# Relative attention: the sheared bias stored, loaded and waited for tile by tile

## The chip, the cores and the metric

One core of one Trainium2 chip runs the whole program. The metric is the device time of one execution in microseconds (us). Five engines run their own instruction streams and meet only through counters (semaphores): TensorE (PE in the profile), VectorE (DVE), ScalarE (ACT), GpSimd (POOL) and SyncE (SP), which here only issues DMA transfers. "PE waits for a counter" means that its stream stands still, in order, until another engine or a landed transfer has raised it.

## What is computed

The program is an audio tower: a token convolution and then four layers, each an attention and a feed-forward part. The change touches one part, the attention of layer 0, with a learned bias that depends on the distance of two positions:

```python
qkv = group_norm(x @ W_qkv, gn_qkv_scale, gn_qkv_bias)      # 4 batches, 8 heads, L = 746 positions
rel_idx = jnp.arange(L)[:, None] - jnp.arange(L)[None, :] + (L - 1)
rpe = rel_emb[:, rel_idx]                                   # rpe_q, rpe_k, rpe_v are its parts
logits = (jnp.einsum('bhdi,bhdj->bhij', q, k) + jnp.einsum('bhdi,dij->bhij', q, rpe_k)
          + jnp.einsum('bhdi,dij->bhij', k, rpe_q))
attn = jax.nn.softmax(logits, axis=3)
out = (jnp.einsum('bhij,bhdj->bhdi', attn, v) + jnp.einsum('bhij,dij->bhdi', attn, rpe_v))
```

## The kernel before

`rel_attention` works through 32 pairs (batch, head). A pair is 6 tiles of 128 query rows (`T = 6`). The bias of row i at column j depends only on j - i, and only 4 tiles (`NS = SKEW_TILES = 4`) and the last 510, 382, 254 and 126 columns of them (`SKEW_W`) have one that differs from a constant. So TensorE makes it unsheared (`position`, L783, into the one bank `x_ps`), ScalarE copies it out (`copy_position`, L887, into `r_sb`), SyncE stores it to a scratch tensor in device memory (L721) and loads it back with a row step that is one short, which shifts each row by one (L735, into four buffers `bias[slot][t]`). VectorE adds it to the scores (L949), takes the row maximum (L953), ScalarE exponentiates (L909), VectorE scales by the reciprocal sum (L931, L933). The probabilities make the same trip in the other direction (L703 stores, L745 loads into `shear`), TensorE transposes both (`turn_probs` L807, `turn_shear` L820), ScalarE and VectorE copy the transposes out, and TensorE multiplies with the values (L834) and the value embedding (L845, the last work of a pair).

Three pairs are in flight. A call `body(new, now, old)` is one turn: `new` gets its bias (position products, stores, loads), `now` its scores and softmax, `old` its output. Two sets of buffers (`slot`) alternate, and every second turn also copies and stores the output of two pairs (L939 on VectorE, L710 on SyncE, four transfers). On each engine the order within a turn is written by hand and strictly kept. In a turn TensorE does in step t: transposes of tile t - 2, scores of tile t + 1, position product t, and from step 2 on parts of `old`. The scores of tile 0 of the next pair are issued in step 5, ahead of L820, L834 and L845. VectorE does in step t: add bias t (t < 4), maximum t, scale t - 1, copy of half a transpose (t >= 2).

Before the change SyncE stores all four tiles of a pair on one counter (`bias_out[slot]`), waits until all four have landed, then issues the four loads on one counter (`bias_in[slot]`), and VectorE waits for all four loads ahead of its first add:

```python
                if new is not None:
                    sp.wait_ge(bias_out[new.slot], new.turn * (16 * NS) + 16 * NS)
                    ...
                    for t in range(NS):
                        sp.dma_start(bias[new.slot][t][:], sheared("rel_bias", new.slot, t, SKEW_ROW - 1, SKEW_W[t])
                                     ).then_inc(bias_in[new.slot], 16)
```

`apart(eng, passed)` raises a counter that nobody waits for; it stands between two waits on one engine so that each has an instruction of its own.

## Time and profile before

| | |
|---|---|
| median of 3 runs | 3236.6 us (3222.63 to 3237.94) |
| profiled execution, its own time | 3237.81 us |
| its span in the profile | 3236.0 us |
| mean granted TensorE clock, whole span | 0.864 |
| relative attention, from the first position product (156.77 us) to the last output store issued (717.43 us) | 561 us of the span |

The span is the time between the first and the last instruction that the profiler saw; the execution's own time is 1.8 us longer. Times in rows are us from the start of the span. The granted clock is 1.00 at 2.4 GHz and 0.50 at 1.2 GHz. An idle time in brackets stands ahead of the instruction that ended it, with what released it. Idle time of an engine that others do not wait for costs nothing.

### The profile page before, as it was taken

How to read it: one execution, taken by the hardware profiler on the slowest of the kernel's cores; microseconds unless marked ns; L12 is line 12 of the kernel's file. 1: busy time of each engine (PE TensorE's matmuls, PEld its weight loads, DVE VectorE, ACT ScalarE, POOL GpSimd, SP SyncE). 2: the span in 40 equal slices, each digit the busy share in tenths (PEclk: the TensorE clock that was granted, in tenths of full speed). 3: DMA queues.
4: the chain of work that ended last, by engine and by line, in shares of the span. 5: the costliest groups of instructions: out<-in, count | busy, mean ns of one | idle time of the engine just before them, and what ended most of it. 6: DMA issues, size and time to landing. Idle time of an engine off the chain costs nothing. (4 is left out here: it accounts for less than half of the span.)

```text
span 3236.0 us, 47690 instructions
## 1 busy us (share of the span) xinstructions
PE 2579.5 (80%) x16218; PEld 1748.2 (54%) x16266; DVE 1705.1 (53%) x3666; ACT 1330.0 (41%) x2799; POOL 203.7 (6%) x240
## 2 busy tenths in 40 slices
PE   5389999975579947867886999998599999962973
PEld 3245555543467846644463666664366666642862
DVE  3477888753306503451353777776476767641113
ACT  2156777652104401433451554554155555531321
POOL 0000000000310040000000000000100000005022
PEclk8578999886789968877996999999699999975986
DMA  2345555542204510001004121320332323102651
GB/s 80 114 153 166 171 181 175 175 129 88 95 20 159 161 34 2 2 1 40 15 1 150 41 101 71 121 92 1 90 87 68 78 66 80 31 9 79 213 162 47
DMA packets 166565, 286.92 MB, mean 89 GB/s; under 512 B 44652, under 2 KB 125924, under 8 KB 162292
## 3 DMA queue, kind: packets, MB, share of 16 engines
q1 hardware_dynamic: 152900, 262.80, 25.7%
q0 software_dynamic: 6144, 12.60, 1.3%
q10 hardware_dynamic: 7360, 9.44, 1.0%
q8 instruction: 93, 1.52, 0.2%
q14 instruction: 68, 0.56, 0.1%
HBM read 167.71 MB, written 79.86 MB: 77 GB/s over the span
## 5 line engine op out<-in xcount | busy, mean ns | idle before, releaser
L2969 ACT ACTIVATE lstm_gate<-lstm_g_ps,lstm_bias 128x373 f32<-128x373 f32 x368 | 210.1, 574 | 251.2 <-PE lstm_g_ps L2930 236.4
L3568 DVE TENSOR_REDUCE caus_nmx<-caus_a_ps 128x4 f32<-128x512 f32 (+5 forms) x352 | 215.9, 642 | 106.2 <-PE caus_a_ps L3384 103.4
L2930 PE MATMUL lstm_g_ps<-lstm_state,lstm_w 128*128 128x373 f32 x640 | 254.7, 480 | 6.7 <-DVE lstm_state L3052 4.1
L3519 ACT ACTIVATE caus_probsT<-caus_s_ps 128x512 f32<-128x512 f32 (+4 forms) x352 | 189.7, 559 | 150.5 <-PE caus_s_ps L3403 147.0
L807 PE MATMUL rel_t_ps<-tower_ident,rel_probs 128*128 128x128 f32 x1152 | 189.1, 307 | 40.0 <-DVE rel_probs L933 36.5
L436 PE MATMUL moe_hb<-moe_z_part,moe_w1h 128*128 x576 | 156.4, 349 | 63.0 <-issue 53.3
L2924 PE MATMUL lstm_g_ps<-lstm_xm,lstm_w 128*128 128x373 f32 x512 | 202.3, 477 | 0.0
L953 DVE TENSOR_REDUCE rel_nmax<-rel_s_ps 128x1 f32<-128x746 f32 x192 | 179.0, 932 | 20.2 <-PE rel_s_ps L792 13.2
L3384 PE MATMUL caus_a_ps<-caus_ks,caus_qs 96*128 96x128 f32 (+6 forms) x768 | 180.6, 327 | 10.6 <-DVE caus_nmx L3568 10.4
L807 PEld LDWEIGHTS rel_t_ps<-tower_ident,rel_probs 128*128 128x128 f32 x1152 | 144.1, 156 | 80.4 <-DVE rel_probs L933 53.6
L3403 PE MATMUL caus_s_ps<-caus_qs,caus_ks 98*128 98x128 f32 (+6 forms) x768 | 186.4, 333 | 0.5 <-ACT caus_probsT L3519 0.4
L909 ACT ACTIVATE rel_probs<-rel_s_ps,rel_nmax 128x746 f32<-128x746 f32 x192 | 171.5, 893 | 22.2 <-DVE rel_rsum L931 11.9
L2930 PEld LDWEIGHTS lstm_g_ps<-lstm_state,lstm_w 128*128 128x128 f32 x640 | 122.1, 191 | 87.1 <-DVE lstm_state L3052 4.7
L696 ACT COPY rel_probsT<-rel_t_ps 128x384 f32<-128x384 f32 x256 | 117.4, 486 | 125.1 <-PE rel_t_ps L807 123.2
L436 PEld LDWEIGHTS moe_hb<-moe_z_part,moe_w1h 128*128 128x128 f32 x576 | 109.6, 199 | 67.9 <-issue 67.3
L3403 PEld LDWEIGHTS caus_s_ps<-caus_qs,caus_ks 98*128 98x128 f32 (+1 forms) x768 | 122.7, 190 | 34.5 <-issue 21.8
L3384 PEld LDWEIGHTS caus_a_ps<-caus_ks,caus_qs 96*128 96x128 f32 (+1 forms) x768 | 122.3, 191 | 30.3 <-DVE caus_nmx L3568 23.8
L1779 DVE SCALAR_TENSOR_TENSOR stage_y<-moe_ob,moe_b,tower_zT 128x373 f32<-128x373 f32 x8 | 4.8, 605 | 249.2 <-PE moe_ob L1579 249.2
L2203 ACT ACTIVATE moe_hid<-moe_hb,moe_w 128x256 f32<-128x256 f32 x152 | 62.4, 471 | 179.3 <-PE moe_hb L2139 91.4
L2924 PEld LDWEIGHTS lstm_g_ps<-lstm_xm,lstm_w 128*128 128x128 f32 x512 | 97.3, 190 | 63.1
L436 PE MATMUL moe_hb<-moe_z_part,moe_w1l 128*128 x288 | 99.9, 347 | 28.5 <-issue 28.5
L933 DVE TENSOR_SCALAR rel_probs<-rel_probs,rel_rsum 128x746 f32<-128x746 f32 x192 | 117.0, 609 | 6.8
(477 smaller groups left out, 5080.5 us busy)
## 6 DMA issues: line engine op xcount, KB each, us to landing
lstm_row<-gates SPq DMA_DIRECT2D x16, 1536.0 KB, 13.7
moe_w<-in_moe_w SPq DMA_DIRECT2D x38, 578.0 KB
moe_ew<-in_moe_w SPq DMA_DIRECT2D x33, 578.0 KB
caus_qs<-caus_xh SPq DMA_DIRECT2D x128, 93.2 KB, 2.1
caus_ks<-caus_xh SPq DMA_DIRECT2D x128, 93.2 KB, 2.1
lstm_row<-gates SPq DMA_DIRECT2D x8, 1152.0 KB, 7.3
moe_x<-moe_xs SPq DMA_DIRECT2D x71, 128.0 KB
moe_ys<-moe_yo SPq DMA_DIRECT2D x71, 128.0 KB, 1.7
```

What stands on the lines that cost most here:

```text
L436: mm = nc.tensor.matmul(out, w[i], x[j], start=(start and n == 0), stop=(stop and n == len(terms) - 1))
L696: copy(probsT[pair.slot][:, j0:j0 + T // 2, t * P:(t + 1) * P], t_ps[i][:, 0:T // 2 * P].rearrange("p (j i) -> p j i", i=P)).then_inc(t_co ...
L807: mm = nc.tensor.transpose(t_ps[i][:, j * P:(j + 1) * P], probs[pair.slot][:, t, k * P:(k + 1) * P], K["ident"][:])
L909: nc.scalar.activation(probs[now.slot][:, t, 0:L], s_ps[t % 2][:, 0:L], ACT.Exp, bias=nmax[now.slot][:, t:t + 1], accum_out=sums[now.slot] ...
L953: nc.vector.tensor_reduce(nmax[now.slot][:, t:t + 1], s_ps[t % 2][:, 0:L], AX.X, ALU.max, negate=True).then_inc(max_ready, 1)
L2924: mm = nc.tensor.matmul(bank, w[e % 2][:, g * P:(g + 1) * P], z, start=True, stop=(s == 0))
L2930: mm = nc.tensor.matmul(bank, w[e % 2][:, 4 * P + g * P:4 * P + (g + 1) * P], state[e % 2][k or 0][i][:], start=False, stop=True)
L2969: nc.scalar.activation(gate[x % 3][g][:], g_ps[n % RING][:, 0:HALF], ACT.Tanh if g == 2 else ACT.Sigmoid, bias=b[:, e, g:g + 1]).then_inc( ...
L3384: mm = nc.tensor.matmul(out[:, at, :], qs[s][0:K_S, hh, t * P:q1], ks[s][0:K_S, hh, k0:k1], start=not diag, stop=not diag or hh == HPG - 1)
L3403: mm = nc.tensor.matmul(out[:, at, :], ks[s][0:K_T, hh, j * P:k1], qs[s][0:K_T, hh, q0:q1], start=not diag, stop=not diag or hh == HPG - 1)
L3519: nc.scalar.activation(probsT[j][0:rows, heads[0]:heads[-1] + 1, q0 - j * P:q1 - j * P], heads_of(s_ps[at % 3][0:rows, :], heads, q1 - q0) ...
L3568: nc.vector.tensor_reduce(nmx[0:rows, slot, heads[0]:heads[-1] + 1, t:t + 1], heads_of(bank[0:rows, :], heads, k1 - k0), AX.X, ALU.max, ne ...
```

## The change

Each tile gets counters of its own. SyncE stores tile t, and then, once the store of tile t - 1 has landed, issues the load of tile t - 1; the last load comes behind the last store of probabilities. VectorE waits ahead of each of the four adds for that tile alone, ScalarE ahead of each of its four copies for the store that last read that part of `r_sb`. The wait for all four scores of `old` ahead of the loads is dropped; each load waits for `old`'s add of the same tile. The bytes moved and the work of all engines are the same. VectorE, ScalarE and SyncE get `apart` instructions and waits in each turn.

```diff
--- before.py
+++ after.py
@@ -650,7 +650,8 @@
         x_ps = a.ps("x_ps", [P, BANK])
         o_ps = a.ps("o_ps", [P, BANK])
         in_sem = a.sems("pair_in", 2)
-        bias_out, bias_in = a.sems("bias_out", 2), a.sems("bias_in", 2)
+        bias_out = [a.sems(f"bias_out{i}_", SKEW_TILES) for i in range(2)]
+        bias_in = [a.sems(f"bias_in{i}_", SKEW_TILES) for i in range(2)]
         probs_out, shear_in = a.sems("probs_out", 2), a.sems("shear_in", 2)
         t_copied = a.sems("t_copied", 2)
         names = ("r_full", "r_copied", "a_full", "a_copied", "s_full", "max_ready", "exp_done", "rs_ready",
@@ -703,6 +704,14 @@
                 sp.dma_start(scratch["rel_probs"][now.slot, t, :, 0:SKEW_W[t]],
                              probs[now.slot][:, t, L - SKEW_W[t]:L]).then_inc(probs_out[now.slot], 16)
 
+            def load_bias(new, old, t):
+                sp.wait_ge(bias_out[new.slot][t], new.turn * 16 + 16)
+                if old is not None:
+                    apart(sp, passed)
+                    sp.wait_ge(biased, old.n * ADDED + t + 1)
+                sp.dma_start(bias[new.slot][t][:], sheared("rel_bias", new.slot, t, SKEW_ROW - 1, SKEW_W[t])
+                             ).then_inc(bias_in[new.slot][t], 16)
+
             def store_output(turn):
                 sp.wait_ge(o_copied, turn + 1)
                 for q, c0 in enumerate(QUARTERS):
@@ -711,31 +720,27 @@
                                  o_sb[q * 2 * HD:(q + 1) * 2 * HD, 0:c1 - c0]).then_inc(o_stored, 16)
 
             def body(new, now, old):
-                if old is not None and new is not None:
-                    sp.wait_ge(bias_in[new.slot], new.turn * (16 * NS))
                 if old is not None and now is not None and not now.early:
                     sp.wait_ge(shear_in[now.slot], now.turn * (16 * NS))
+                    apart(sp, passed)
                 for t in range(NS):
                     if new is not None:
+                        if old is not None:
+                            sp.wait_ge(bias_in[new.slot][t], new.turn * 16)
+                            apart(sp, passed)
                         sp.wait_ge(r_copied, new.n * NS + t + 1)
                         sp.dma_start(scratch["rel_bias"][new.slot, t, :, 0:SKEW_W[t]], r_sb[new.slot][:, t, 0:SKEW_W[t]]
-                                     ).then_inc(bias_out[new.slot], 16)
+                                     ).then_inc(bias_out[new.slot][t], 16)
+                        if t > 0:
+                            load_bias(new, old, t - 1)
                     if now is not None and t > 0:
                         store_probs(now, t - 1)
                     if t == 2 and old is not None and old.slot == 0 and not old.first:
                         store_output(old.turn - 1)
-                if new is not None:
-                    sp.wait_ge(bias_out[new.slot], new.turn * (16 * NS) + 16 * NS)
-                    apart(sp, passed)
-                    if old is not None:
-                        sp.wait_ge(s_full, old.n * T + NS)
-                        apart(sp, passed)
-                        sp.wait_ge(biased, old.n * ADDED + ADDED)
-                    for t in range(NS):
-                        sp.dma_start(bias[new.slot][t][:], sheared("rel_bias", new.slot, t, SKEW_ROW - 1, SKEW_W[t])
-                                     ).then_inc(bias_in[new.slot], 16)
                 if now is not None:
                     store_probs(now, NS - 1)
+                if new is not None:
+                    load_bias(new, old, NS - 1)
                 if now is not None:
                     sp.wait_ge(probs_out[now.slot], now.turn * (16 * NS) + 16 * NS)
                     apart(sp, passed)
@@ -881,8 +886,9 @@
                 act.dma_start(rhs[pair.slot][:], scratch["rel_rhs"][bass.ds(pair.n, 1), :, :].squeeze(0)).then_inc(in_sem[pair.slot], 16)
 
             def copy_position(new, old, t):
-                if t == 0 and old is not None:
-                    act.wait_ge(bias_out[new.slot], new.turn * (16 * NS))
+                if old is not None:
+                    act.wait_ge(bias_out[new.slot][t], new.turn * 16)
+                    apart(act, passed)
                 act.wait_ge(r_full, new.n * NS + t + 1)
                 nc.scalar.copy(r_sb[new.slot][:, t, 0:SKEW_W[t]], x_ps[:, 0:SKEW_W[t]]).then_inc(r_copied, 1)
 
@@ -943,8 +949,8 @@
                     if now is not None:
                         dve.wait_ge(s_full, now.n * T + t + 1)
                         if t < ADDED:
-                            if t == 0:
-                                dve.wait_ge(bias_in[now.slot], now.turn * (16 * NS) + 16 * NS)
+                            apart(dve, passed)
+                            dve.wait_ge(bias_in[now.slot][t], now.turn * 16 + 16)
                             corner = s_ps[t % 2][:, L - SKEW_W[t]:L]
                             nc.vector.tensor_tensor(corner, corner, bias[now.slot][t][:], ALU.add).then_inc(biased, 1)
                             dve.wait_ge(biased, now.n * ADDED + t + 1)
```

SyncE, the straight-line turn behind the loop (pair 31 is `new`), before: `rel_r_sb` to `rel_bias` is a store of the bias, `rel_probs` to `rel_probs` a store of probabilities, `rel_bias_t` a load of tile t.

```order
L721 DMA rel_bias<-rel_r_sb 128x510 [waits rel_r_copied,rel_shear_in0,rel_bias_in1]
L721 DMA rel_bias<-rel_r_sb 128x382 [waits rel_r_copied]
L703 DMA rel_probs<-rel_probs 128x510 [waits rel_scaled]
L721 DMA rel_bias<-rel_r_sb 128x254 [waits rel_r_copied]
L703 DMA rel_probs<-rel_probs 128x382 [waits rel_scaled]
L721 DMA rel_bias<-rel_r_sb 128x126 [waits rel_r_copied]
L703 DMA rel_probs<-rel_probs 128x254 [waits rel_scaled]
L735 DMA rel_bias_0<-rel_bias 128x510 [waits rel_bias_out1,rel_s_full,rel_biased]
L735 DMA rel_bias_1<-rel_bias 128x382
L735 DMA rel_bias_2<-rel_bias 128x254
L735 DMA rel_bias_3<-rel_bias 128x126
L703 DMA rel_probs<-rel_probs 128x126 [waits rel_scaled]
```

The same turn, changed:

```order
L732 DMA rel_bias<-rel_r_sb 128x510 [waits rel_shear_in0,rel_bias_in1_0,rel_r_copied]
L732 DMA rel_bias<-rel_r_sb 128x382 [waits rel_bias_in1_1,rel_r_copied]
L712 DMA rel_bias_0<-rel_bias 128x510 [waits rel_bias_out1_0,rel_biased]
L704 DMA rel_probs<-rel_probs 128x510 [waits rel_scaled]
L732 DMA rel_bias<-rel_r_sb 128x254 [waits rel_bias_in1_2,rel_r_copied]
L712 DMA rel_bias_1<-rel_bias 128x382 [waits rel_bias_out1_1,rel_biased]
L704 DMA rel_probs<-rel_probs 128x382 [waits rel_scaled]
L732 DMA rel_bias<-rel_r_sb 128x126 [waits rel_bias_in1_3,rel_r_copied]
L712 DMA rel_bias_2<-rel_bias 128x254 [waits rel_bias_out1_2,rel_biased]
L704 DMA rel_probs<-rel_probs 128x254 [waits rel_scaled]
L704 DMA rel_probs<-rel_probs 128x126 [waits rel_scaled]
L712 DMA rel_bias_3<-rel_bias 128x126 [waits rel_bias_out1_3,rel_biased]
```

The load of tile 0 has moved from behind all stores of the bias to behind the second, ahead of the first store of probabilities, and waits for one landing; loads 1 and 2 stand each behind the next store, load 3 behind the last store of probabilities.

VectorE, the third turn (pair 1 is `now`), steps 0 to 2, before:

```order
L949 TENSOR_TENSOR rel_s_ps<-rel_s_ps,rel_bias_0 128x510 [waits rel_bias_in1,rel_s_full]
L953 TENSOR_REDUCE rel_nmax<-rel_s_ps 128x1 [waits rel_biased]
L931 RECIPROCAL rel_rsum<-rel_sums 128x1 [waits rel_exp_done]
L933 TENSOR_SCALAR rel_probs<-rel_probs,rel_rsum 128x746 [waits rel_rs_ready]
L949 TENSOR_TENSOR rel_s_ps<-rel_s_ps,rel_bias_1 128x382 [waits rel_s_full]
L953 TENSOR_REDUCE rel_nmax<-rel_s_ps 128x1 [waits rel_biased]
L931 RECIPROCAL rel_rsum<-rel_sums 128x1 [waits rel_exp_done]
L933 TENSOR_SCALAR rel_probs<-rel_probs,rel_rsum 128x746 [waits rel_rs_ready]
L949 TENSOR_TENSOR rel_s_ps<-rel_s_ps,rel_bias_2 128x254 [waits rel_s_full]
```

And changed:

```order
L955 TENSOR_TENSOR rel_s_ps<-rel_s_ps,rel_bias_0 128x510 [waits rel_s_full,rel_bias_in1_0]
L959 TENSOR_REDUCE rel_nmax<-rel_s_ps 128x1 [waits rel_biased]
L937 RECIPROCAL rel_rsum<-rel_sums 128x1 [waits rel_exp_done]
L939 TENSOR_SCALAR rel_probs<-rel_probs,rel_rsum 128x746 [waits rel_rs_ready]
L955 TENSOR_TENSOR rel_s_ps<-rel_s_ps,rel_bias_1 128x382 [waits rel_s_full,rel_bias_in1_1]
L959 TENSOR_REDUCE rel_nmax<-rel_s_ps 128x1 [waits rel_biased]
L937 RECIPROCAL rel_rsum<-rel_sums 128x1 [waits rel_exp_done]
L939 TENSOR_SCALAR rel_probs<-rel_probs,rel_rsum 128x746 [waits rel_rs_ready]
L955 TENSOR_TENSOR rel_s_ps<-rel_s_ps,rel_bias_2 128x254 [waits rel_s_full,rel_bias_in1_2]
```

Nothing has moved; the first add waits for one tile's counter, and the second and third (and the fourth, below) have a wait for a landing of their own beside that for the scores. The counter instructions of `apart` are not listed in this view.

## Rows read from the trace of the kernel before

**Rows 1.** Window: length, busy PE, PEld, DVE, ACT, POOL, clock, DMA share, GB/s.

```profile
160.00:720.00 560.00, 497.73 (x4093) 283.83 (x4093) 429.41 (x848) 375.41 (x894) 8.60 (x30) 0.88 0.52 164
```

**Rows 2.** Waits of the stage: us in total, times, longest.

```profile
DVE rel_s_ps L949 <- DMA rel_bias<-rel_bias: 76.0, 32, 12.7
PE rel_t_ps L807 <- DVE rel_probs L933: 36.5, 55, 2.2
```

**Rows 3.** Timeline, VectorE, end of one turn: start us, us, instruction, idle before.

```profile
421.11 0.55 DVE L696 COPY rel_probsT<-rel_t_ps 128x384 f32<-128x384 f32 x1
423.28 0.70 DVE L949 TENSOR_TENSOR rel_s_ps<-rel_s_ps,rel_bias 128x510 f32<-128x510 f32 x1 [1.62 <-DMA rel_bias<-rel_bias]
```

**Rows 4.** Timeline, SyncE's DMA issues, one turn.

```profile
411.66 2.33 SPq L721 DMA_DIRECT2D rel_bias<-rel_r_sb  x2
417.17 0.32 SPq L721 DMA_DIRECT2D rel_bias<-rel_r_sb  x1
419.04 1.75 SPq L735 DMA_DIRECT2D rel_bias<-rel_bias  x4
423.57 1.74 SPq L745 DMA_DIRECT2D rel_shear<-rel_probs  x4
```

**Rows 5.** Timeline, TensorE, the same turn and a row of the next.

```profile
408.14 0.87 PE L807 MATMUL rel_t_ps<-tower_ident,rel_probs 128*128 128x128 f32 x6
410.68 0.88 PE L807 MATMUL rel_t_ps<-tower_ident,rel_probs 128*128 128x128 f32 x6 [0.80 <-DVE rel_probs L933]
412.83 0.87 PE L807 MATMUL rel_t_ps<-tower_ident,rel_probs 128*128 128x128 f32 x6 [0.59 <-DVE rel_probs L933]
423.86 0.87 PE L807 MATMUL rel_t_ps<-tower_ident,rel_probs 128*128 128x128 f32 x6
429.93 0.66 PE L820 MATMUL rel_x_ps<-tower_ident,rel_shear 128*128 128x128 f32 x4
```

**Rows 6.** DMA issues by line: KB each, median us to landing.

```profile
rel_bias<-rel_r_sb SPq DMA_DIRECT2D x32, 255.0 KB, 2.0
rel_bias<-rel_bias SPq DMA_DIRECT2D x32, 255.0 KB, 2.6
```

**Rows 7.** Timeline, VectorE, then TensorE, a turn whose bias came early.

```profile
552.27 0.70 DVE L949 TENSOR_TENSOR rel_s_ps<-rel_s_ps,rel_bias 128x510 f32<-128x510 f32 x1 [0.48 <-DMA rel_bias<-rel_bias]
555.74 0.56 DVE L949 TENSOR_TENSOR rel_s_ps<-rel_s_ps,rel_bias 128x382 f32<-128x382 f32 x1 [1.00 <-PE rel_s_ps L792]
...
554.40 0.87 PE L807 MATMUL rel_t_ps<-tower_ident,rel_probs 128*128 128x128 f32 x6
558.04 0.87 PE L807 MATMUL rel_t_ps<-tower_ident,rel_probs 128*128 128x128 f32 x6 [0.39 <-DVE rel_probs L933]
569.33 0.88 PE L807 MATMUL rel_t_ps<-tower_ident,rel_probs 128*128 128x128 f32 x6
```

**Rows 8.** Timeline, TensorE: L845 of the first and the 31st pair.

```profile
200.30 1.36 PE L845 MATMUL rel_o_ps<-rel_shearT,rel_relv_pad 128*32 128x187 f32 x18
706.66 1.36 PE L845 MATMUL rel_o_ps<-rel_shearT,rel_relv_pad 128*32 128x187 f32 x18 [0.72 <-ACT rel_shearT L918]
```

**Rows 9.** Windows of 4 us, columns as in Rows 1.

```profile
341.00:345.00 4.00, 3.06 (x18) 1.51 (x17) 3.77 (x8) 3.03 (x8) 0.27 (x1) 1.00 0.58 179
345.00:349.00 4.00, 3.53 (x18) 1.80 (x19) 3.90 (x8) 2.65 (x7) 0.00 (x0) 0.52 0.48 180
554.40:558.40 4.00, 3.43 (x22) 2.05 (x22) 2.94 (x7) 3.41 (x8) 0.27 (x1) 1.00 0.56 188
```

**Rows 10.** Timeline, VectorE, the projection: an instruction behind a counter instruction.

```profile
125.35 0.21 DVE L461 BATCH_NORM_AGGREGATE relproj_qk_work<-relproj_qk_stats 128x2 f32<-128x12 f32 x1 [0.15 <-DVE relproj_qk_stats L459]
```

**Rows 11.** Timeline, start of the stage: SyncE, then VectorE.

```profile
158.00 2.89 SPq L721 DMA_DIRECT2D rel_bias<-rel_r_sb  x4
162.91 1.74 SPq L735 DMA_DIRECT2D rel_bias<-rel_bias  x4
...
167.17 0.70 DVE L949 TENSOR_TENSOR rel_s_ps<-rel_s_ps,rel_bias 128x510 f32<-128x510 f32 x1 [12.68 <-DMA rel_bias<-rel_bias]
```

## Prediction

> **What bounds the kernel now.** I read the page first, then the windows over the attention stage, the chain of waits inside it, and the timelines of VectorE, SyncE and TensorE side by side for single turns. The program is one of many stages in a row, with barriers between them, so the change is worth what it takes out of this one. In the stage no engine is full: of 560 us TensorE is busy 497.7, VectorE 429.4, ScalarE 375.4, and the granted clock averages 0.88, which is 0.24 x 560 = 134 us at 1.2 GHz [rows 1]. The wait list names the one wait that is no mutual one of the engines: VectorE stands 76.0 us, once in each of the 32 pairs, until the sheared bias has landed; TensorE in turn stands 36.5 us for probabilities that VectorE scaled late [rows 2].
>
> The timelines show how the two hang together. VectorE starts its last copy of a turn at 421.11 and is done 0.55 later; the first add of the next turn starts at 423.28, 1.62 us late [rows 3]. SyncE issued the last store of the bias at 417.17, waited for it to land, and issued the four loads at 419.04 to 420.79 [rows 4]; a load lands 2.6 us after its issue [rows 6], the last one thus at about 423.3. So the first add, which needs tile 0 only, waits for tile 3's round trip. TensorE pays for it two steps on: it stands 0.80 and 0.59 us ahead of the transposes of steps 1 and 2, and that turn is 423.86 - 408.14 = 15.72 us long [rows 5].
>
> The idle time of VectorE is not what can be won. From step 3 to the end of a turn TensorE has hardly a gap: its work, not VectorE's, sets the pace there. What a turn takes when the bias isn't late can be read in this very trace. In the turn at 552 us VectorE waited 0.48 us for the bias; it then waited 1.00 us for TensorE's scores instead, TensorE waited 0.39 us ahead of step 2 and nothing ahead of step 1, and the turn took 569.33 - 554.40 = 14.93 us [rows 7].
>
> All turns together are longer: from the first pair's last products to the 31st's are 30 turns in 706.66 - 200.30 = 506.36 us, 16.88 us each [rows 8]. The 1.16 us over the 15.72 of a turn at full clock are mostly falls of the clock. Before one of them TensorE had been busy 3.06 of 4.00 us, in the steps in which it waits for VectorE; then the clock stood at 0.52 and the work went on at half speed. In the turn without a late bias the same steps had TensorE busy for 3.43 of 4.00 us, and the clock stayed at 1.00 [rows 9]. TensorE: Matmul & The Clock Gate, in the Trainium skill, says under "What's actually happening" that the half clock is the default state and that activity releases it; by this rule too, shorter waits of TensorE would bring back some of the half-clock time, and these rows agree as far as two turns can show it.
>
> **The change, part by part.**
>
> Load 0 goes from behind the fourth store to behind the second. In the shown turn the first two stores were issued from 411.66 to 413.99 [rows 4]; store 0 lands 2.0 us after its start [rows 6], at 413.7, so SyncE doesn't wait, load 0 goes out at about 414.1 and lands at 416.7. VectorE is free for it at 421.66. It has 5 us of cover. Load 1 waits for store 1, load 2 stands behind store 3 (417.17), load 3 behind the last store of probabilities, which in the old order goes out between 420.8 and 423.6 [rows 4] and in the new one earlier. Load 3 lands by 424 to 426 even so, and the fourth add comes three of six steps, some 7 us, after the first. All four are hidden, and the wait of [rows 2] goes in every turn. If the cover were gone, a tile would cost what it does now, 1.6 to 2.2 us of VectorE.
>
> What is late next is TensorE: VectorE waits for the scores of tile 1 and the turn is 14.93 us instead of the mean 16.88: 1.95 us x 30 turns = 58.5 us. This takes it that no fall of the clock is left.
>
> The added instructions: per turn four counter instructions and three more waits on VectorE, four on ScalarE. The nearest row is an instruction behind such a counter instruction on VectorE, which started 0.15 us after its predecessor's end [rows 10]. Most of this lies under idle time (VectorE waits 1.00 us for scores in step 1). On the path from TensorE's step 0 to its step 3 lie at most three of them: VectorE's second and third add and ScalarE's copy of position 1. From below 0 (the queue takes them while an instruction runs), from above 3 x 0.15 = 0.45 us per turn. I take 0.1: 3 us in 30 turns, 0 to 13.5 in the range. VectorE: DVE Perf Modes, in the Trainium skill, says under "The DRAIN you can't avoid" that a semaphore after each operation costs nothing extra; by that this term would be 0. The row has 0.15 us where a counter instruction and a second wait stand, so the page doesn't decide it.
>
> The start: the first add waits until 167.17, for the bias alone; the four stores went out from 158.00, the four loads from 162.91, behind the landing of all stores [rows 11]. Load 0 can go out once store 0 has landed, at about 160.3, and lands by 163.1: 4 us, none of it hidden, since no other pair is at work. The second turn's wait shrinks as well; I count nothing for it (0 to 2).
>
> SyncE's queue: behind each new wait for a landing stand a store of probabilities and the next store of the bias, and behind all of them the loads of `shear`. Four loads of 0.44 us go from one place to four others, so the queue has no more to issue. The wait for the last store moves behind the last store of probabilities, whose own landing is awaited there anyway. Nothing of it is on the path while `shear` lands in time: in the shown turn the last load is issued by 425.3 [rows 4] and lands at 428.1 (2.8 us, for a smaller piece of the same kind a little over [rows 6]), TensorE takes it at 429.93 [rows 5], 1.8 us later. I expect it earlier against the turn, since the stores of probabilities no longer wait behind the loads of the bias.
>
> Sum, against the profiled execution's own 3237.8 us (1.2 above the median): -58.5 + 3 - 4 = -59.5, 3178.3. One or two falls will stay, at the start at least; a turn with one is some 2 us longer than 15.72 (18 us, since (16.88 - 15.72) x 30 = 35 us are spread over some 15 turns). I forecast 3180 us.
>
> **The rivals.**
>
> The clock keeps falling. The turn is 15 us without a fall, but TensorE still waits 0.4 us ahead of step 2, and which stretch a fall catches may be chance. Were all 35 us of it to stay, the time would be 3180 + 35 = 3215. For it: only few turns in the trace had an early bias. Against: those that had it kept full clock [rows 7, 9].
>
> TensorE sets the pace anyway and the wait only changes its name: VectorE stands for TensorE and the turn stays near 15.7, the mean near 16.9: 3234. For it: TensorE is busy 89% of the stage [rows 1]. Against: the turn of 14.93 us is a turn of the same work.
>
> Slower: SyncE's waits chain up and `shear` comes late. Each turn has four waits for a landing of up to 2.0 us [rows 6] in the middle of SyncE's stream, 8 us if none finds its store landed. TensorE would stand ahead of L820 once the last `shear` load is 1.8 us later than now, and since the turn becomes 1.95 us shorter the change loses from 3.75 us on. At 6 us the turn would be 14.93 + 4.2 = 19.1 us and the time 3237.8 + 2.25 x 30 = 3305. Against: stores 0 and 1 start 2 us apart, so two of four waits are nearly over when they are reached, and the fourth is shared with that for the probabilities. DMA: Bandwidth & Descriptors, in the Trainium skill, says under "Anatomy of one DMA" that a wait is done by the issuing sequencer ahead of the transfer and that completion takes most of 2 us; this is the rule by which this rival works, and the landing of 2.0 us here agrees with it.
>
> **How the numbers follow.** Main case 0.70, its own range 3168 to 3196 (counter instructions 0 to 13.5 us, start 2 us more, up to four falls left). The clock keeps falling, in half of the cases or more: 0.18, 3197 to 3218. TensorE sets the pace anyway: 0.08, 3222 to 3245. Slower by SyncE: 0.04. The range of 8 in 10 takes the main case and most of the second: 3166 to 3214. This kernel's measurement tells about 0.5% (16 us) from no change: the first two cases are faster but for the top of the second, which makes 0.87; the third is mostly no change, 0.09; slower 0.04.
>
> **What the new profile would show.** VectorE's wait for the bias gone from the list (76 to under 5 us), and in its place some 1 us a turn for TensorE's scores; turns of 14.9 to 15.1 us between L845 and the next; no wait of TensorE in step 1 and about 0.4 in step 2; a granted clock above 0.95 in the stage after the first turns; the first add at about 163; SyncE's loads of tile 0 about 7 us ahead of the add. The prediction is wrong if the bias wait stays in any step, if TensorE waits ahead of L820 for `shear`, or if the half clock stays at some 100 us.

## The result

The changed kernel took 3173.62 us, the median of 4 runs (3170.41 to 3176.54). The kernel before, run beside it, took 3229.61 us (3213.63 to 3237.94, 4 runs). The ratio is 0.9845, with a 95% interval of 0.9808 to 0.9881: faster by 1.6%. The profiled execution took 3170.41 us, its span 3168.8 us.

First the windows of the changed kernel (length, busy PE, PEld, DVE, ACT, POOL, clock, DMA share, GB/s): the stretch of [rows 1], the 500 us in which all its turns lie, 29 whole turns by themselves, and the first 4 us of a turn, which answer to [rows 9]. The last line is the kernel before, its 29 turns.

```profile
160.00:720.00 560.00, 474.10 (x4194) 274.66 (x4193) 450.29 (x905) 382.38 (x916) 8.05 (x30) 0.92 0.58 168
160.00:660.00 500.00, 453.76 (x4092) 261.85 (x4090) 425.12 (x848) 369.14 (x893) 8.05 (x30) 0.97 0.63 183
196.50:632.80 436.30, 403.57 (x3714) 233.12 (x3712) 384.30 (x768) 333.22 (x812) 7.78 (x29) 1.00 0.65 190
408.61:412.61 4.00, 3.33 (x21) 1.95 (x21) 2.73 (x6) 3.42 (x8) 0.27 (x1) 1.00 0.67 221
...
201.90:690.80 488.90, 445.11 (x3714) 254.15 (x3712) 388.60 (x768) 338.85 (x812) 8.34 (x30) 0.90 0.54 171
```

The stage now ends about 60 us earlier, so that the first row reaches into what comes behind it; the second has a clock of 0.97 against 0.87 in the same stretch before. In the turns alone the clock is 1.00 against 0.90; what is missing in the 500 us lies ahead of the first turn. At the start of a turn TensorE is busy for 3.33 of 4.00 us. In [rows 9] it was 3.06 ahead of a fall of the clock and 3.43 in the turn with an early bias. The two are not far apart: from 408.14 to 412.14 in the kernel before, in a turn without a fall, it was 3.15. So these windows don't show what lets the clock fall; the experiment with filler below does.

The waits of the stage (us in total, times, longest), against [rows 2]:

```profile
DVE rel_s_ps L955 <- PE rel_s_ps L797: 41.5, 34, 2.2
PE rel_x_ps L788 <- DMA rel_rhs<-rel_rhs: 15.7, 20, 3.1
PE rel_t_ps L812 <- DVE rel_probs L939: 10.6, 21, 0.9
DVE rel_s_ps L955 <- DMA rel_bias<-rel_bias: 9.1, 1, 9.1
PE rel_x_ps L825 <- DMA rel_shear<-rel_probs: 1.6, 1, 1.6
```

VectorE waits for the bias once, in the very first turn; in the others it waits 1.2 us for the scores of tile 1. TensorE has a wait of 0.8 us in 20 of the turns for the load of the next pair's operands; before it had one of 0.7 us in 8 turns.

VectorE from one turn to the next, then the first add of the stage:

```profile
408.24 0.61 DVE L939 TENSOR_SCALAR rel_probs<-rel_probs,rel_rsum 128x746 f32<-128x746 f32 x1
410.05 0.56 DVE L955 TENSOR_TENSOR rel_s_ps<-rel_s_ps,rel_bias 128x382 f32<-128x382 f32 x1 [1.20 <-PE rel_s_ps L797]
...
420.63 0.55 DVE L697 COPY rel_probsT<-rel_t_ps 128x384 f32<-128x384 f32 x1
421.09 0.69 DVE L955 TENSOR_TENSOR rel_s_ps<-rel_s_ps,rel_bias 128x510 f32<-128x510 f32 x1
...
162.96 0.70 DVE L955 TENSOR_TENSOR rel_s_ps<-rel_s_ps,rel_bias 128x510 f32<-128x510 f32 x1 [9.10 <-DMA rel_bias<-rel_bias]
```

SyncE, against [rows 4]:

```profile
414.05 0.32 SPq L712 DMA_DIRECT2D rel_bias<-rel_bias  x1
415.05 0.32 SPq L732 DMA_DIRECT2D rel_bias<-rel_r_sb  x1
415.56 0.37 SPq L712 DMA_DIRECT2D rel_bias<-rel_bias  x1
416.69 0.32 SPq L732 DMA_DIRECT2D rel_bias<-rel_r_sb  x1
418.17 0.32 SPq L712 DMA_DIRECT2D rel_bias<-rel_bias  x1
420.05 0.32 SPq L712 DMA_DIRECT2D rel_bias<-rel_bias  x1
421.70 1.75 SPq L750 DMA_DIRECT2D rel_shear<-rel_probs  x4
```

Load 0 goes out at 414.05, 7.0 us ahead of its add at 421.09, and that add follows the copy without a gap. The `shear` loads go out 421.70 - 408.61 = 13.1 us behind the turn's first transposes, where it was 423.57 - 408.14 = 15.4 [rows 4, 5].

TensorE, against [rows 5] and [rows 8]:

```profile
408.61 0.87 PE L812 MATMUL rel_t_ps<-tower_ident,rel_probs 128*128 128x128 f32 x6
409.42 0.48 PE L797 MATMUL rel_s_ps<-rel_rhs,rel_lhs 48*128 48x512 bf16 x2
410.23 0.82 PE L812 MATMUL rel_t_ps<-tower_ident,rel_probs 128*128 128x128 f32 x6
412.36 0.87 PE L812 MATMUL rel_t_ps<-tower_ident,rel_probs 128*128 128x128 f32 x6 [0.56 <-DVE rel_probs L939]
423.38 0.87 PE L812 MATMUL rel_t_ps<-tower_ident,rel_probs 128*128 128x128 f32 x6
...
194.90 1.36 PE L850 MATMUL rel_o_ps<-rel_shearT,rel_relv_pad 128*32 128x187 f32 x18
646.30 1.35 PE L850 MATMUL rel_o_ps<-rel_shearT,rel_relv_pad 128*32 128x187 f32 x18 [0.72 <-ACT rel_shearT L924]
```

This turn is 423.38 - 408.61 = 14.77 us; the next is 15.0, and so on by turns. Thirty of them take 646.30 - 194.90 = 451.40 us, 15.05 us each, against 16.88.

**Where the 67 us came from.** The profiled executions differ by 3237.81 - 3170.41 = 67.4 us. The 30 turns give 506.4 - 451.4 = 55.0, what lies ahead of the first L845 or L850 gives 200.30 - 194.90 = 5.4, and 7.0 lie outside. Behind the last turn the ten traces below that are not from chip B differ by up to 16 us among themselves (2529 to 2545 us from the last turn's copy of V to the end), whatever the kernel, so nothing is to be read into the 7.0.

### The profile page after: what moved, and what is told of

Its sections match the earlier page's. It is cut to its first block and busy times, and to the rows that moved or that the text cites. A ratio compares the mean times of both kernels' runs of the same rounds, so it can differ in the third digit from the quotient of the medians.

```text
span 3168.8 us, 48207 instructions
## 1 busy us (share of the span) xinstructions
PE 2526.6 (80%) x16218; PEld 1723.2 (54%) x16266; DVE 1700.1 (54%) x3666; ACT 1323.8 (42%) x2799; POOL 202.6 (6%) x240
## 5 line engine op out<-in xcount | busy, mean ns | idle before, releaser
L812 PE MATMUL rel_t_ps<-tower_ident,rel_probs 128*128 128x128 f32 x1152 | 170.3, 286 | 14.8 <-DVE rel_probs L939 10.6
L812 PEld LDWEIGHTS rel_t_ps<-tower_ident,rel_probs 128*128 128x128 f32 x1152 | 128.9, 145 | 51.1 <-issue 28.9
```

The source lines that it names most:

```text
L812: mm = nc.tensor.transpose(t_ps[i][:, j * P:(j + 1) * P], probs[pair.slot][:, t, k * P:(k + 1) * P], K["ident"][:])
```

## The experiments

In what follows "a turn" is read from one place in every trace, GpSimd's copy of V (`rel_v_pad`), which waits for the last products of a pair: 30 copies, 29 turns. The table has all traces. "Typical" is the median of the 29 turns; "fallen" counts the turns whose granted clock, taken from copy to copy, is under 0.97. Nearly all others have 1.00. The last column also has the 35 to 40 us ahead of the first turn, with a clock of about 0.6, and in e8_both 52 us behind the last.

| kernel | chip | time, us | ratio, 95% interval | mean turn | typical | fallen | clock 160:660 |
|---|---|---|---|---|---|---|---|
| before, first trace | | 3229.61 | | 16.86 | 15.73 | 12 | 0.87 |
| changed, first trace | | 3173.62 | 0.9845 (0.9808 to 0.9881) | 15.04 | 15.03 | 1 | 0.97 |
| e1_counters | B | 3019.04 | 0.9875 (0.9845 to 0.9905) | 15.01 | 14.95 | 1 | 0.96 |
| e2_one_wait | B | 3037.90 | 0.9926 (0.9890 to 0.9962) | 15.96 | 15.12 | 5 | 0.91 |
| e3_filler | B | 3039.69 | 0.9935 (0.9910 to 0.9960) | 15.62 | 15.55 | 0 | 0.97 |
| e4_at_once | B | 3156.55 | 1.0326 (1.0293 to 1.0360) | 19.50 | 20.22 | 21 | 0.82 |
| c_after (changed) | C | 3171.99 | 0.9870 (0.9832 to 0.9908) | 15.07 | 15.03 | 1 | 0.97 |
| e5_bias_first | C | 3160.67 | 0.9843 (0.9808 to 0.9878) | 14.84 | 14.92 | 0 | 0.97 |
| e6_exp_first | C | 3181.48 | 0.9902 (0.9871 to 0.9932) | 15.28 | 15.04 | 3 | 0.96 |
| e8_both | C | 3143.99 | 0.9800 (0.9761 to 0.9840) | 14.26 | 14.12 | 0 | 0.95 |
| k_before (before) | D | 3213.92, one run | | 16.19 | 15.59 | 7 | 0.92 |
| k_counters | D | 3170.00 | 0.9879 (0.9857 to 0.9901) | 15.06 | 14.96 | 1 | 0.96 |
| k_after (changed) | D | 3167.36 | 0.9867 (0.9843 to 0.9891) | 15.07 | 15.04 | 1 | 0.96 |
| k_scores_bias_first | D | 3168.31 | 0.9869 (0.9846 to 0.9893) | 15.04 | 14.92 | 3 | 0.96 |

The kernel before took 3064.34 us on chip B (15 runs), 3209.59 on C (8) and 3208.83 on D (11), so times are compared within a chip only. The turns can be compared: the changed kernel and the counters alone have 15.01 to 15.07 us on all four. In the first trace of before the 12 fallen turns take 18.92 us in the mean and the 17 others 15.40.

### The counters alone

SyncE as before (four stores, one place to wait, four loads), but with a counter for each tile on VectorE, ScalarE and SyncE.

```diff
-                        if t > 0:
-                            load_bias(new, old, t - 1)
...
+                if new is not None:
+                    for t in range(NS):
+                        sp.wait_ge(bias_out[new.slot][t], new.turn * 16 + 16)
+                        apart(sp, passed)
+                    for t in range(NS):
+                        if old is not None:
+                            sp.wait_ge(biased, old.n * ADDED + t + 1)
+                        sp.dma_start(bias[new.slot][t][:], sheared("rel_bias", new.slot, t, SKEW_ROW - 1, SKEW_W[t])
+                                     ).then_inc(bias_in[new.slot][t], 16)
```

> The changed kernel with SyncE's old order: all four stores of the bias, the wait until all four have landed, then the four loads in a row, then the last store of probabilities. Only the counters and VectorE's waits are per tile. My theory (the wait per tile counts, and TensorE hides what is left): load 0 goes out at about the place of 419.04 in the old trace, lands 2.6 us later at about 421.6, when VectorE comes free, and up to 1 us of lateness is hidden by VectorE's wait for scores 1; turns of 14.9 to 15.2 us, first add at about 165.5 instead of 163, 3174 to 3186 us. Rival (the place of the loads counts): VectorE still stands 1.5 to 2 us a turn, half-clock time stays, 3215 to 3235 us.

It has the whole gain: turns of 15.01 us, inside the 14.9 to 15.2 expected, and a ratio of 0.9875. Since the chip was another, it was run again beside the changed kernel:

> Counters for each tile alone, SyncE's order as before: again, beside the changed kernel on one chip. Theory A (the single wait for the last of four transfers was what cost; the earlier loads by themselves give nothing more once TensorE sets the pace): turns of 15.0 us as in the changed kernel, and a time within 0.3% of it. Theory B (the earlier loads are worth something too): 10 to 20 us slower than the changed kernel.

> The changed kernel, unchanged, as the measure for the other three on the same chip: turns of 15.0 to 15.1 us, a ratio to the kernel before of 0.983 to 0.988, and the only wait for the bias of over 1 us that of the first turn.

3170.00 against 3167.36 us, 15.06 against 15.07 us a turn: no difference that can be told, as theory A said. VectorE's waits in that trace:

```profile
DVE rel_s_ps L960 <- PE rel_s_ps L802: 31.2, 33, 1.4
DVE rel_s_ps L960 <- DMA rel_bias<-rel_bias: 18.3, 16, 11.0
```

In 15 turns a rest of the wait for the bias is left, (18.3 - 11.0) / 15 = 0.5 us each. It comes out of the 1.2 us for which VectorE would stand for the scores of tile 1 anyway (41.3 us in the changed kernel on this chip, 31.2 here), and costs nothing. Load 0 by itself is hardly late in the old order: it lands as VectorE comes to it or half a microsecond after. The three behind it were what the one counter made it wait for.

### The new order alone

The changed kernel, with all four waits ahead of the first add.

```diff
-                            apart(dve, passed)
-                            dve.wait_ge(bias_in[now.slot][t], now.turn * 16 + 16)
+                            if t == 0:
+                                for k in range(NS):
+                                    apart(dve, passed)
+                                    dve.wait_ge(bias_in[now.slot][k], now.turn * 16 + 16)
```

> The changed kernel, but VectorE waits for all four tiles of the bias ahead of its first add; SyncE's order is the new one. My theory: the last load goes out at about 420.05 in the changed kernel's trace and lands 2.0 to 2.8 us later, 1 to 1.8 us after VectorE would have begun; about 1 us of that is hidden behind TensorE, so turns of 15.0 to 15.6 us and 3175 to 3195 us. Rival (only the wait per tile counts): the full old wait is back, 3215 to 3235 us. Rival (only the order counts): equal to the changed kernel, 3170 to 3177 us.

```profile
DVE rel_s_ps L957 <- DMA rel_bias<-rel_bias: 49.4, 25, 12.2
DVE rel_s_ps L957 <- PE rel_s_ps L797: 17.0, 28, 2.7
```

Part of the gain, and less than expected: turns of 15.96 us (15.0 to 15.6 expected), of which 5 are fallen; the typical turn is 15.12. The wait is now for tile 3's load, which stands behind the last store of probabilities. It comes somewhat earlier than the four of before: the wait is (49.4 - 12.2) / 24 = 1.55 us in 24 turns, where it was (76.0 - 12.7) / 31 = 2.04 in 31 [rows 2]. The order of the transfers gives 26 of the 45 us that the counters give on this chip, and on top of them nothing that can be told. One price of it shows in the waits: TensorE stands for the next pair's operands (`rel_rhs`) 20 to 27 times in the three traces of the changed kernel, 0.8 us each, and 3 and 8 times in the two with the counters alone. Whether the order would give something without that was not tried.

### The wait kept, the clock held up

The kernel before, with three transposes of the identity into a bank that is overwritten afterwards, ahead of each of the two places where TensorE waits in steps 1 and 2. They are added work, six products a turn, in TensorE's idle time.

```diff
-            def turn_probs(pair, t):
+            def turn_probs(pair, t, fill=0):
+                if fill:
+                    pe.wait_ge(t_copied[0], pair.n * T + t)
+                    for _ in range(fill):
+                        nc.tensor.transpose(t_ps[0][:, 0:P], K["ident"][:], K["ident"][:])
                 pe.wait_ge(scaled, pair.n * T + t + 1)
...
+            FILL = 3
...
-                        turn_probs(pair, tile)
+                        turn_probs(pair, tile, FILL if now is not None and old is not None and t in (1, 2) else 0)
```

> The kernel before, with three extra transposes of the identity on TensorE ahead of its waits for probabilities in steps 1 and 2 of each full turn (their result is overwritten). They fill idle time and leave the bias as late as it was. My theory (some 35 us of the old time are falls of the clock, brought about by TensorE's short idle times): granted clock of the stage from 0.88 to above 0.94, turns of 15.5 to 15.8 us instead of 16.88, 3195 to 3212 us, VectorE's wait for the bias unchanged at 60 to 76 us. Rival (the falls have another cause): clock as before, and time 0 to 15 us longer for the added work, 3230 to 3252 us.

Its window, and its wait for the bias in the same 500 us:

```profile
160.00:660.00 500.00, 464.95 (x4098) 270.56 (x4099) 416.17 (x834) 363.24 (x872) 8.01 (x30) 0.97 0.57 180
```

```profile
DVE rel_s_ps L954 <- DMA rel_bias<-rel_bias: 75.6, 32, 12.6
```

The wait is whole (75.6 us, where the kernel before has 69.9 in this window), but the clock is at 0.97 in the window and 1.00 in all 29 turns, and the turn is 15.62 us. So what lets the clock fall in the kernel before is TensorE's idle time in steps 1 and 2. This splits the loss. Of the 1.82 us a turn between before and the changed kernel, 16.86 - 15.62 = 1.24 went with the falls of the clock and 15.62 - 15.04 = 0.58 is the late bias as such. The typical turns say the same: 15.73 and 15.59 in the two traces of before, 15.55 with filler, 15.03 changed. So do the medians on chip B, which need no trace: 3064.34 - 3039.69 = 24.7 us go with the filler, and 3039.69 - 3019.04 = 20.7 more with the counters.

The kernel before had its trace taken once more, on the chip of `k_after`:

> The kernel before, unchanged, once more with its trace, on the chip of the three runs that follow. In the first trace of it the relative part's turns took 16.86 us each between the copies of V (first at 201.9, last at 690.8, 29 turns), with a granted clock of 0.87 from 160 to 660 us. On the chip of the first four experiments the whole kernel was 5% shorter. If the clock of the other stages makes that difference and the turns are alike, they take 16.6 to 17.0 us here too; if this chip lets the clock fall less often behind the wait for the bias, they take 15.7 to 16.5 and the early bias has less to give back.

```profile
160.00:660.00 500.00, 444.67 (x3773) 252.53 (x3773) 402.13 (x798) 352.11 (x843) 7.74 (x29) 0.92 0.56 176
```

The same program, the same wait for the bias (73.1 us in 31 turns of this window), but 7 fallen turns in place of 12, and 16.19 us in the mean, the second of the two cases expected. There the change takes (16.19 - 15.07) x 30 = 34 us from the turns where the first pair of traces had 55. So what the change is worth depends on how often the clock would have fallen, which varies from one trace to the next of an unchanged kernel. The ratios, 0.9845 once and 0.987 twice, have intervals that overlap and don't show it by themselves. Whether it is the chip or chance that lets the clock fall more or less often was not tried.

### Each load right behind its store

The rival in which SyncE's waits chain up, made on purpose: load t waits for store t at once.

```diff
-                        if t > 0:
-                            load_bias(new, old, t - 1)
+                        load_bias(new, old, t)
...
-                if new is not None:
-                    load_bias(new, old, NS - 1)
```

> The changed kernel with each load right behind its own store, so that SyncE stands for each landing (2 us) with the stores of probabilities queued behind it. My theory: SyncE is 2 to 4 us later at the end of a turn; the shear loads then land at about the moment TensorE wants them, later in every second turn, which has four stores of the output as well: 0 to 2 us of TensorE's wait for shear in half of the turns, 3173 to 3205 us. Rival of my prediction (SyncE's waits chain up): shear late in all turns, 3220 us or more. Rival (SyncE has room to spare): equal to the changed kernel, 3170 to 3177 us.

SyncE's turn, then what TensorE waits for (same kernel):

```profile
424.24 0.32 SPq L732 DMA_DIRECT2D rel_bias<-rel_r_sb  x1
427.33 0.32 SPq L712 DMA_DIRECT2D rel_bias<-rel_bias  x1
428.30 0.32 SPq L732 DMA_DIRECT2D rel_bias<-rel_r_sb  x1
431.04 0.32 SPq L712 DMA_DIRECT2D rel_bias<-rel_bias  x1
439.05 1.27 SPq L747 DMA_DIRECT2D rel_shear<-rel_probs  x3
...
443.24 0.76 PE L822 MATMUL rel_x_ps<-tower_ident,rel_shear 128*128 128x128 f32 x4 [2.61 <-DMA rel_shear<-rel_probs]
```

These two loads go out 3.1 and 2.7 us behind their stores (2.2 to 3.2 in the eight of two turns), and nothing else moves on SyncE meanwhile. The loads of `shear` come late, and TensorE stands for them 24 times, 70.0 us, with a clock of 0.82 and 21 fallen turns. The kernel is 3.3% slower: neither the 0 to 2 us in half of the turns nor equality, but the rival. One place in the queue, load t - 1 in place of load t, is all that lies between this and the change. Behind the next store the landing has mostly come when SyncE asks for it: in the 500 us SyncE waits for stores of the bias 105 times here, 229 us, and 46 times in the changed kernel, 37 us.

### The counter instruction

VectorE's wait for the bias, and the counter instruction, ahead of the wait for the scores.

```diff
-                        dve.wait_ge(s_full, now.n * T + t + 1)
                         if t < ADDED:
-                            apart(dve, passed)
                             dve.wait_ge(bias_in[now.slot][t], now.turn * 16 + 16)
+                            apart(dve, passed)
+                        dve.wait_ge(s_full, now.n * T + t + 1)
+                        if t < ADDED:
```

> The changed kernel with VectorE's two waits ahead of an add in the other order: first the one for the bias (long landed), then the counter instruction, then the one for the scores on the add itself. My theory: the counter instruction costs 0.11 us only where VectorE really waits, which is once a turn for scores 1; the gap between the end of scores 1 and the add falls from 0.15 to 0.04 us, the turn from 14.9 to 14.8 us, 3 to 4 us in all. Rival (counter instructions cost nothing anywhere): no difference, 0 us. Rival (they cost on every add): 10 us or more.

> The changed kernel unaltered, as the control for its variants on the same chip. 3170 to 3177 us; turns of 14.77 and 15.03 us in turn.

In the changed kernel the scores of tile 1 are done at 409.42 + 0.48 = 409.90 and the add starts at 410.05, 0.15 us later. Here:

```profile
417.16 0.49 PE L797 MATMUL rel_s_ps<-rel_rhs,rel_lhs 48*128 48x512 bf16 x2
417.68 0.56 DVE L956 TENSOR_TENSOR rel_s_ps<-rel_s_ps,rel_bias 128x382 f32<-128x382 f32 x1 [1.16 <-PE rel_s_ps L797]
```

0.03 us. The same gap is 0.14 to 0.16 us in all of these waits of the changed kernel from 200 to 620 us, and 0.03 to 0.05 in all of them here. It is 0.03 to 0.05 in e2_one_wait too, where no counter instruction and no second wait stand ahead of the add of tile 1. So a counter instruction and the wait behind it cost 0.12 us where they come behind the wait that really holds the engine. Where VectorE doesn't stand, nothing of it shows: the add at 421.09 above follows the copy without a gap. The typical turn goes from 15.03 to 14.92. The medians differ by 11.3 us, of which 30 x 0.11 = 3.3 are the counter's. The turns of the two traces differ by 29 x 0.225 = 6.5 us in all, since none is fallen here; the rest lies outside them.

### The next bound: a ring over three engines

VectorE's new wait of 1.2 us is for TensorE, which in step 0 does the transposes ahead of the scores of tile 1. Two remedies, the diffs cut to the calls that move: ScalarE's first exponential ahead of its copies of step 0,

```diff
                 for t in range(T):
+                    if now is not None and t == 0:
+                        exponent(now, t)
                     pair, tile = turning(now, old, t)
```

> The changed kernel with ScalarE's exponential of tile 0 ahead of the copies of the old pair's transposes, in the 1.92 us in which ScalarE stands idle at the start of a turn. My theory: the exponential is off ScalarE's busy stretch, but probabilities 0 wait for VectorE's step 1, which waits for TensorE's scores 1: TensorE's wait ahead of step 2 stays at 0.4 to 0.6 us, turn 0 to 0.2 us shorter, 3165 to 3174 us. Rival (ScalarE is what holds the turn): 0.5 us or more a turn, 3158 us or less.

or TensorE's scores of tile 1 ahead of the transposes (together with the bias wait first, as above),

```diff
                     pair, tile = turning(now, old, t)
+                    if now is not None and t == 0:
+                        scores(now, t + 1)
                     if pair is not None:
                         turn_probs(pair, tile)
```

> The changed kernel with TensorE's scores of tile 1 ahead of the transposes in step 0 and VectorE's wait for the bias ahead of its wait for the scores; ScalarE's first exponential stays where it is. Theory A (TensorE's order alone is what keeps VectorE waiting 1.2 us in each turn; moving the exponential only delays ScalarE's copies, as its run by itself showed): turns of 14.1 to 14.4 us, as short as with all three moves or shorter, 20 to 28 us below the changed kernel. Theory B (the exponential of tile 0 must be early too, or the maximum and exponential of tile 1 come too late for the gain): turns of 14.6 to 14.9 us, 5 to 12 us below the changed kernel.

and all of them:

> The changed kernel with ScalarE's exponential of tile 0 first, TensorE's scores of tile 1 ahead of the transposes in step 0, and VectorE's bias wait ahead of its score wait. My theory: VectorE's step 1 begins 0.8 us earlier, TensorE's wait ahead of step 2 goes, and the turn is 14.3 to 14.6 us; 3152 to 3163 us. Rival (TensorE's own work is the bound already): 14.8 us, 3168 to 3174 us.

Neither remedy shortens the turn by itself, and neither expectation held: 3181.48 us (3165 to 3174 expected), 9.5 above the changed kernel on its chip, though the intervals overlap, and 3168.31, 1.0 above it, where both theories had at least 5 us below. The second includes the bias wait first; its typical turn is 14.92 us, what that wait gives alone. All three moves together give 28.0 us, of which the turns have (15.07 - 14.26) x 30 = 24, somewhat more than expected (3152 to 3163 us), and a ratio of 0.980 to before, the lowest of the study. Against e5_bias_first, on the same chip, the two remedies give 3160.67 - 3143.99 = 16.7 us. The exponential first was not run together with the bias wait first, so that it gives nothing is known only without it. Three traces show how the wait moves. With the exponential first, VectorE's wait stays, since TensorE's scores come where they came, and ScalarE gets a wait for VectorE:

```profile
408.73 0.89 ACT L902 ACTIVATE rel_probs<-rel_s_ps,rel_nmax 128x746 f32<-128x746 f32 x1 [1.15 <-DVE rel_rsum L942]
410.36 0.56 DVE L960 TENSOR_TENSOR rel_s_ps<-rel_s_ps,rel_bias 128x382 f32<-128x382 f32 x1 [1.21 <-PE rel_s_ps L797]
```

With the scores first, the add is on time, but the transposes come later, ScalarE's copies wait 2.34 us for them (1.9 at most in the changed kernel), the exponential stands behind the copies, and VectorE now waits for its sum:

```profile
419.14 0.86 ACT L697 COPY rel_probsT<-rel_t_ps 128x384 f32<-128x384 f32 x2 [2.34 <-PE rel_t_ps L812]
...
418.67 0.56 DVE L960 TENSOR_TENSOR rel_s_ps<-rel_s_ps,rel_bias 128x382 f32<-128x382 f32 x1 [0.40 <-PE rel_s_ps L797]
420.91 0.16 DVE L941 RECIPROCAL rel_rsum<-rel_sums 128x1 f32<-128x1 f32 x1 [0.71 <-ACT rel_probs L919]
```

With both, the exponential runs in the time in which ScalarE would wait for the transposes, and the turn is 14.12 us:

```profile
409.34 0.88 ACT L906 ACTIVATE rel_probs<-rel_s_ps,rel_nmax 128x746 f32<-128x746 f32 x1 [1.06 <-DVE rel_rsum L946]
...
410.15 0.56 DVE L965 TENSOR_TENSOR rel_s_ps<-rel_s_ps,rel_bias 128x382 f32<-128x382 f32 x1 [0.36 <-PE rel_s_ps L797]
```

## Why the prediction was right

It was 3180 us in a range of 3166 to 3214; measured were 3173.62. The mechanism is the one forecast, but that the size came out so close is in part luck. The forecast takes 57.8 us from the profiled execution of the kernel before, 3237.81 us, as slow as the slowest of its four runs (3237.94), with 12 fallen turns. The medians differ by 56.0 us here, by 37.6 on chip C and by 41.5 on chip D. By its own steps:

- **The bias wait goes in every turn, load 0 with 5 us of cover.** Right: 9.1 us once, at the start, and from then on load 0 lands at about 414.05 + 3.0 = 417.1, ahead of VectorE's copy that ends at 421.18. ("Under 5 us" in the list of signs contradicts the prediction's own start: 12.68 us less 4 leaves 8.7.) The reason given, that the add of tile 0 waited for tile 3's round trip, is what the counters alone confirm. That load 0 must also be issued earlier, as the step has it, is not so: the old order with four counters has the same turns.
- **TensorE sets the pace next, 14.93 us, 58.5 us in 30 turns.** 15.05 and 55.0 us. Both the turn read from the trace of before and the new wait (1.00 us predicted, 1.2 found) were there in advance, in one turn that happened to have its bias early. That the turns of the changed kernel alternate between 14.77 and 15.03 us wasn't seen.
- **No fall of the clock left, then one or two.** One fallen turn, at a clock of 0.90, and 1.00 in the others. The prediction put 0.79 us a turn to the wait (15.72 - 14.93) and 1.16 to the clock; the filler measures 0.58 and 1.24. It spread the falls over some 15 turns of 18 us; there were 12 of 18.92. The rival in which the clock keeps falling is refuted for this kernel: the five traces of the changed kernel and of the counters alone have 1 fallen turn of 29 each, e5, e6, e8 and k_scores_bias_first 0 to 3. With filler in steps 1 and 2 and the bias as late as ever there is none, so it is TensorE's idle time in these steps that lets the clock fall, and the early bias takes most of it away: the wait for probabilities goes from 36.5 to 10.6 us.
- **Counter instructions, 0.1 us a turn.** 0.11, at one of the three places named, VectorE's second add. Most of the counter instructions do lie under idle time; this one doesn't, since it comes behind the wait for scores. The sentence of VectorE: DVE Perf Modes in the Trainium skill that the prediction names, that a semaphore costs nothing extra, is about one that an operation raises. What costs 0.12 us here is an instruction of its own with a wait behind it, so the runs neither bear the sentence out nor contradict it.
- **The start, 4 us.** 5.4, of which the first add has 167.17 - 162.96 = 4.2.
- **SyncE's queue, nothing.** The loads of `shear` went out 2.3 us earlier in the turn, and TensorE waited for them once, 1.6 us. The rival was real all the same, one place further up in the queue. That it has 19.5 us a turn where the rival gave 19.1 is chance: the rival had 4.2 us of waiting a turn at full clock, the trace has 24 waits of 2.9 us, and 21 of 29 turns are fallen. The 2 us that the prediction names beside it, from "Anatomy of one DMA" in DMA: Bandwidth & Descriptors, in the Trainium skill, stand there for transfers issued by GpSimd. Here SyncE issues them: in the kernel before its stores of the output (23 KB) landed after 1.4 to 1.5 us, those of the bias (63 to 255 KB) after 1.5 to 2.0.
- **The steps that the list named.** TensorE waited 0.56 us ahead of step 2 (0.4 predicted) and nothing ahead of step 1; the first add came at 162.96 (163).

Not foreseen: many landings became longer. The store of 255 KB is unchanged; the load of 255 KB takes 3.0 us in place of the 2.6 of [rows 6], the store of 255 KB of probabilities 3.2 in place of 2.1, and the operands of the next pair 3.0 in place of 2.5. The load of 63 KB became shorter, 2.0 in place of 3.0. With the counters alone, in the old order, they are 2.6, 2.1, 2.3 to 2.4 and 2.9 us, so it is the new order that changes them:

```profile
rel_bias<-rel_r_sb SPq DMA_DIRECT2D x32, 255.0 KB, 2.0
rel_bias<-rel_bias SPq DMA_DIRECT2D x32, 255.0 KB, 3.0
rel_rhs<-rel_rhs ACTq DMA_DIRECT2D x31, 72.0 KB, 3.0
```

With 7 us of cover it cost the bias nothing. For the operands it makes TensorE's 20 waits of 0.8 us; what they cost a turn isn't known.

## What to carry to other kernels

Where several transfers share a counter, the first to be used waits for the last; here a counter for each was worth more than an earlier issue, and a wait for a landing in a queue belongs one transfer further down, not right behind its store. A stall on one engine can cost twice: here a half (in one trace of before) to two thirds (in the other) of what the turns lost was falls of TensorE's clock that came with the stall, and added work in the gaps shows which part is which. When a turn runs in a ring over several engines, moving one link only moves the wait: try the moves together before giving up one of them, and run each pair too, so that it is known which of them are needed.

## What the runs showed of the hardware

The kernel before took 3064 us on chip B and 3209 to 3230 in the other three comparisons, while the turns of this stage, with the counters alone, took 15.01 us on chip B and 15.06 on chip D. From the last turn to the end, the same kernel (counters alone) took 2388 us on chip B and 2529 on chip D, and 99 of these 141 us are one wait, in the mixture of experts. Chip D, then chip B, waits from 700 to 1600 us:

```profile
DVE stage_y L1790 <- PE moe_ob L1590: 250.3, 7, 90.8
```

```profile
DVE stage_y L1790 <- PE moe_ob L1590: 151.5, 7, 40.6
```

Whether its weights' transfers or something else is slower on the other chips was not tried.
